# One mask operation for four heads in place of two for two heads each, in the second softmax of a single-core language-model block

## The reference, cut to what matters

```python
attn = softmax(einsum('bnd,bmd->bnm', q, k) * scale)
out = einsum('bnm,bmd->bnd', attn, v)
...                                             # projection, then unit tokens per head
sim = einsum('bnd,bmd->bnm', sim_tokens, sim_tokens) * 10.0
sim = where(sim < 0, -inf, sim)                 # the mask
sim = softmax(sim)
out2 = einsum('bnm,bmd->bnd', sim, v)           # same v
```

## Time and profile before

| what | us |
|---|---|
| median of 3 runs | 648.37 |
| lowest, highest of them | 639.27, 650.65 |
| the profiled execution | 639.4 |
| its span, first to last instruction | 637.6 |

### The profile page before, as it was taken

The page is one execution under the profiler, slowest core; times in us unless marked ns, Lnnn a source line. Parts: engine busy times, 40 slices in busy tenths (PEclk is TensorE's granted clock), DMA queues, the critical chain, the costliest instruction groups (busy, mean ns, idle before and its releaser), DMA issues.

```text
span 637.6 us, 11853 instructions
## 1 busy us (share of the span) xinstructions
PE 538.5 (84%) x3480; PEld 322.5 (51%) x3481; DVE 430.0 (67%) x859; ACT 341.5 (54%) x795; POOL 231.6 (36%) x281
## 2 busy tenths in 40 slices
PE   0658799988999899999998878426999999999990
PEld 0323323433344233533353332415999999999990
DVE  3489987888798999897678987376643434343420
ACT  1132676677788888788977856210333333334340
POOL 6860430417052150103113110003356666656541
PEclk9977999999999999999998999755999999999996
DMA  4182052135534180312333369822133232333321
GB/s 117 45 116 37 25 86 36 30 72 87 64 52 91 22 129 10 65 45 52 50 71 83 54 158 255 265 89 92 18 58 50 51 49 51 48 52 47 54 33 13
DMA packets 40562, 45.00 MB, mean 71 GB/s; under 512 B 10404, under 2 KB 34854, under 8 KB 40519
## 3 DMA queue, kind: packets, MB, share of 16 engines
q0 software_dynamic: 12864, 19.97, 18.5%
q1 hardware_dynamic: 27654, 24.52, 17.6%
HBM read 17.88 MB, written 7.60 MB: 40 GB/s over the span
## 4 chain that ended last, share of the span: by engine, by line
PE 63%; DVE 18%; issue 8%; DMA 6%; ACT 3%; POOL 0%; SPq 0%; POOLq 0%; DVEq 0%; ACTq 0%
PE psum L1121 11%; PE psum L973 10%; PE psum L1105 7%; DVE MX L745 5%; PE psum L1034 5%; PE psum L1010 5%; PE psum L1110 5%; PE psum L1041 4%; PE psum L1026 4%; DVE arena L759 4%; DMA result<-T,slot_dest 4%; PE psum L1063 3%; PE psum L998 2%; PE psum L1052 1%; ACT arena L596 1%
## 5 line engine op out<-in xcount | busy, mean ns | idle before, releaser
L596 ACT ACTIVATE arena<-psum 128x512 f32<-128x512 f32 x384 | 206.9, 615 | 42.5 <-PE psum L1034 27.5
L632 ACT ACTIVATE arena<-psum,b_sb 128x128 f32<-128x128 f32 x234 | 64.6, 375 | 127.2 <-PE psum L1110 127.2
L745 DVE TENSOR_REDUCE MX<-psum 128x1 f32<-128x512 f32 x192 | 123.4, 681 | 8.1 <-PE psum L1026 7.9
L759 DVE SCALAR_TENSOR_TENSOR arena<-arena 128x1024 f32<-128x1024 f32 x96 | 120.4, 1266 | 11.9 <-ACT arena L596 11.5
L973 PE MATMUL psum<-arena 128*17 128x512 f32 x768 | 102.0, 604 | 5.7 <-DVE arena L759 5.7
L511 POOL DMA_INDIRECT result<-T,slot_dest x39 | 68.6, 1759 | 73.8 <-DMA result<-T,slot_dest 50.9
L1121 PE MATMUL psum<-arena 128*128 x468 | 86.3, 335 | 0.0
L369 POOL DMA_DIRECT2D KS<-arena x72 | 36.8, 512 | 118.1 <-PE psum L1041 58.9
L1121 PEld LDWEIGHTS psum<-arena 128*128 128x128 f32 x468 | 75.0, 190 | 4.7
L1026 PE MATMUL psum<-late_stacks,arena 96*128 96x512 bf16 x144 | 57.5, 409 | 12.2 <-DMA late_stacks<-arena 7.3
L1041 PE MATMUL psum<-KS,QS 96*128 96x512 bf16 x192 | 66.4, 386 | 1.0 <-issue 0.5
(11 more groups left out here) (175 smaller groups left out, 643.0 us busy)
## 6 DMA issues: line engine op xcount, KB each, us to landing
late_stacks<-arena POOLq DMA_DIRECT2D x72, 64.0 KB, 4.3
QS<-arena SPq DMA_DIRECT2D x72, 64.0 KB, 3.6
KS<-arena POOLq DMA_DIRECT2D x72, 64.0 KB, 3.6
arena<-w SPq DMA_DIRECT2D x8, 576.0 KB, 8.1
arena<-arena SPq DMA_DIRECT2D x54, 64.0 KB, 4.4
arena<-w SPq DMA_DIRECT2D x8, 384.0 KB, 6.0
x_rows<-X SPq DMA_DIRECT2D x4, 384.0 KB, 2.5
result<-H SPq DMA_DIRECT2D x4, 384.0 KB, 3.1
```

The lines of the kernel that those rows point to most:

```text
L596: act.activation((P1, P2)[ps][:, n % PRING, :], s, ACT.Exp, scale=(QSCALE, SIM_SCALE)[ps]).then_inc(done, 1)
L745: dve.tensor_reduce(MX[:, g % 2, CT * i + c:CT * i + c + 1], slot(k), AX_X, ALU.max).then_inc(freed[k % RING], 1)
L759: dve.scalar_tensor_tensor(p, p, 1.0, p, ALU.is_ge, ALU.mult).then_inc(masked, 1)
```

## The change

The mask operation now takes all four heads of a key chunk, 128 partitions by 2,048 elements. In the schedule it stands where the second of the two operations stood (odd q); the first one's place is empty. It waits for all four exponentials of the chunk. `pv` waits for c + 1 operations of its group instead of 2(c + 1). Nothing moves on the other engines.

```diff
@@ schedule()
-            at(a + OFF_E + q + 1.25, 0, "mask", g, q)
+            if q % 2:
+                at(a + OFF_E + q + 1.25, 0, "mask", g, q // 2)
@@ VectorE
                     elif kind == "mask":
-                        g, q = args
-                        wait_consumed(dve, unit("sim_unit", g, q, 0))
-                        wait_consumed(dve, unit("sim_unit", g, q, 1))
-                        n = 2 * (UG * g + q) % PRING
-                        p = P2[:, n:n + 2, :]
+                        g, c = args
+                        for q in (2 * c, 2 * c + 1):
+                            for j in range(2):
+                                wait_consumed(dve, unit("sim_unit", g, q, j))
+                        n = GH * (CT * g + c) % PRING
+                        p = P2[:, n:n + GH, :]
                         dve.scalar_tensor_tensor(p, p, 1.0, p, ALU.is_ge, ALU.mult).then_inc(masked, 1)
@@ TensorE, before pv of the second softmax
-                            pe.wait_ge(masked, UG * g + 2 * (c + 1))
+                            pe.wait_ge(masked, CT * g + c + 1)
```

## The result

| | median us | lowest, highest | runs |
|---|---|---|---|
| before | 646.93 | 639.27, 650.65 | 4 |
| double mask | 668.55 | 663.97, 669.56 | 4 |

The ratio is 1.035, with a 95% interval of 1.029 to 1.040. The forecast was 652 within 642 to 661, so the change costs some 22 us where I said 5. The profiled executions took 639.4 us (before, its lowest) and 669.6 us (after, its highest).

The account below looks back on a forecast made before the run. VectorE was taken as the limit by a hair in the middle, a mask-to-product chain in groups 8 to 11. Terms 0 + 0 + 5.3 us gave 644.7 on the profiled execution, 653.7 on the median; forecast 652, range 642 to 661.

Parts of the forecast that it names:

- Duration of the double mask: On VectorE: one double mask takes 2.30 us to its own end, 2.22 to the next start.
- Similarities alone: From 344 us on, groups 8 to 11, 16 chunks: later mask ends make products later, +5.3 us by the last product.
- the chain that was worked out: Groups 8 to 11: weights, double mask, product in sequence; in group 8, 5.35 us for two chunks, 2.68 each.
- The middle: To about 293 us, 21 chunks with maxima beside masks: put at 0, between -2.9 and +4 us.
- The loop: Middle: TensorE's tile, maximum, double mask, next maximum, freed matmuls: 4.69 us a chunk, against 4.68 now.
- the ring for maxima: Middle: PSUM tiles that VectorE's maxima free for TensorE, which may be only one step ahead; 4.69 us a chunk.
- The next stretch: Exponentials and similarities, to about 344 us, 11 chunks: mask ends 1.08 us later, under 1.79 to spare, so 0.
- The clock: Group 10: a longer TensorE wait may draw out the dip to the lower clock, up to +2 us.
- the wait in group 10: TensorE's idle time ahead of group 10's second product: from 2.19 us to about 3 us.
- The first rival: Whole kernel: VectorE's saved fixed time counts and later mask ends are hidden, -6.7 us at most; chance 0.28.
- The second rival: Middle: the ring of maxima stalls, from about 0.4 us a chunk, slower by over 2%; chance 0.07.
- Its sign: Middle: a wait for a maximum of 0.5 us or more in each chunk would show the second rival.

Follow-up runs that it names:

- e1: Double masks in groups 0 to 4 only, masks of 1,024 elements elsewhere, against the kernel before: ratio 1.011.
- e8: Every row maximum over 256 instead of 512 elements, with the double mask of the changed kernel: 648.35 us, one execution.
- e4: Two masks of 1,024 elements a chunk as before, both at the second one's place, one right behind the other: ratio 1.028 to before.
- e5: Two masks of 1,024 elements a chunk, the first half a step later than before, one maximum between them: ratio 1.005 to before.
- e2: Double masks in groups 5 to 7 only, masks of before elsewhere, against the kernel before: ratio 1.008.
- e7: Every row maximum over 256 instead of 512 elements, masks as in the kernel before: 633.16 us, one execution.
- e10: Masks of before, but small operations (division, row remainder, unit tokens, residual) go ahead of a mask that shares their schedule time: ratio 1.002 to before.
- e6: Four masks of 512 elements (one head each) a chunk, spread evenly, against the kernel before: ratio 1.002.
- e11: Masks of two heads in groups 0 to 4 as before, of one head each from group 5 on: ratio 0.993 to before.

## Why the prediction was wrong, point by point

- *Duration of the double mask*, 2.30 us: right (2.29). VectorE's busy time down by 3 to 7: right (4).
- *Similarities alone, +5.3*: right, 5.6, and by the chain that was worked out. Chunk by chunk, group 8 lost 1.74 against 1.7, group 9 1.3 against 1.4, group 10 0.7 against 0.55, group 11 1.75 against 1.65.
- *The middle, "4.69 us a chunk, as much as the 4.68", put at 0*: **the step that failed**, +8.9. The loop was right for a chunk with nothing in it but maxima and masks, and e1 shows such chunks at the old pace (the first three products of its group 3 come without any new delay). But VectorE's other work is queued in it: unit tokens, statistics, the division, the row remainder. Whenever one had made VectorE late, the next tile that TensorE wanted stood behind 2.2 us of mask instead of 1.1. I had followed the ring for maxima only, though each group has tiles of other kinds in it (e1, e8), and averaged where few places decide.
- *The next stretch, "under the 1.79 to spare, so 0"*: failed too, +5.4. The spare time is that of the product. The division and the row remainder behind the mask have none: TensorE waited 2.58 us instead of 1.52 for the division, and the exponentials of group 11 now wait 0.9 us for the remainder's transfer. These two are some 2 of the 5.4 us.
- *The clock, "up to +2"*: mis-sized, and looked for in one place only, the wait in group 10. That wait was 2.55 us (forecast near 3) and its dip as long as before. Instead there were three new dips in the middle and a longer low stretch behind the attention, where the 6.1 us are.
- *The first rival, 0.28* (the fixed time wins): no. VectorE's 4 us were saved and no stretch is shorter for it.
- *The second rival, 0.07*: the nearest to what came. Its price, from about 0.4 us a chunk in the middle, is what was measured (8.9 / 21 = 0.42), with the late groups on top. Its sign, a wait for a maximum of 0.5 us or more in each chunk, didn't come: the delays are few and large, and some are for the division and the remainder. That its average fits is in part luck. I had named what speaks for it, a loop with no slack and extra work that adds up in it, and took the average anyway. e4 and e5 show that a long stretch of masks is the cause.
- What stays open: how the 8.9 divide between waits and dips. A dip costs TensorE time in which VectorE catches up, so they can't be added; e1 had one dip and lost 7.3, e8 none and 3.9 with more slack. The lower clock behind the attention was in both profiles of the change but also, in part, in kernels without a late double mask (e2, e7 and e10, 243.4 to 244.5, against 240 in the others), so how much of the 6.1 belongs to the change isn't settled.

## What to carry to other kernels

Merging two operations of an in-order engine saves a fixed time that the rows tell (0.06 us here) and doubles the time in which that engine answers nobody. Before merging, list every operation that stands behind the merged one and hands back a buffer, one-off tiles too, and ask for each how far ahead the waiting engine may run; where two engines are near balance with a ring one step deep, merge none, and put what the other engine waits for between the pieces. Splitting further than before gained nothing in the middle here (e6, +1.4 us). Where a chain of waits rules, a shorter last piece ahead of the waiting engine brings the product forward, by 0.2 us a group here (e6, e11).

## What the runs showed of the hardware

TensorE's granted clock fell to the lower level behind waits of 1.45 and 1.68 us in otherwise busy stretches of after; such a dip shows as eight matmuls in 1.91 instead of 1.05 us. The length of the wait ahead doesn't decide it. Two waits of 1.68 us in e1 (at 206.66 and 284.49) and one of 1.31 in before (211.22) were followed by no dip. Ahead of the second product of group 10 e1 and e2 both wait 1.84 us, and only e1 has a dip behind it. So what a change costs by the clock couldn't be told here from the waits alone. A mask of VectorE and a subtraction of GpSimd, both on tiles in SBUF, stretched each other in e1: the mask from 2.29 to 3.14 us, the subtraction from 1.16 to 2.53.
